# Cross attention in a decoder-like stack: normalisation, queries and attention merged into one block, with the first batch's keys and maxima among them

## The reference, cut to what matters

```
x = x + xattn_0(layernorm(x), ctx)     # Wq, bq, Wk, Wv, bv, Wo, bo
x = x + self_attention(layernorm(x))
x = x + experts(layernorm(x))
x = x + xattn_1(layernorm(x), ctx)     # no biases
x = x + mamba(layernorm(x))
x = x + expert_ffn(layernorm(x))

layernorm(x) = (x - mean) / sqrt(var + 1e-5)
xattn(q, ctx): qh = q @ Wq + bq; kh = ctx @ Wk + bk; vh = ctx @ Wv + bv
               softmax(qh kh^T / 4) vh, heads joined, @ Wo + bo
```

## Time and profile before

| | us |
|---|---|
| median of three runs (range) | 3891.38 (3885.2 to 3892.71) |
| profiled execution, its own time | 3889.54 |
| its span | 3887.8 |
| PE busy (share of the span) | 3490.9 (90%) |
| DVE busy | 2569.8 (66%) |
| ACT busy | 2155.1 (55%) |
| POOL busy | 1468.7 (38%) |
| mean granted TensorE clock | 0.940 |

### The profile page before, as it was taken

How to read it: one execution, slowest core, us unless ns; L and a number is a source line. 1 busy time by engine, 2 the same in 40 slices (tenths; PEclk the granted TensorE clock), 3 DMA queues, 4 the chain that set the end, 5 groups by cost and what they waited for, 6 DMA issues and landing times. The chain is left out here.

```text
span 3887.8 us, 136421 instructions
## 1 busy us (share of the span) xinstructions
PE 3490.9 (90%) x58106; PEld 2894.7 (74%) x58107; DVE 2569.8 (66%) x4398; ACT 2155.1 (55%) x3407; POOL 1468.7 (38%) x1389
## 2 busy tenths in 40 slices
PE   6999999999885399938999999999868899999988
PEld 4888888888674266626888888888438888888867
DVE  5777777777543122236777777777669888889864
ACT  2666666666543022204666666666447788888732
POOL 3333333333131300043333333332018888888700
PEclk8999999999996699968999999999879999999989
DMA  2001000100005201020100010000001111111100
GB/s 69 29 32 35 29 29 29 37 29 20 11 1 206 86 30 32 30 76 31 34 29 29 29 37 29 29 29 12 26 15 48 42 44 42 44 39 44 39 24 22
DMA packets 60394, 148.33 MB, mean 38 GB/s; under 512 B 8194, under 2 KB 28706, under 8 KB 59458
## 3 DMA queue, kind: packets, MB, share of 16 engines
q1 hardware_dynamic: 56770, 131.70, 10.1%
q0 software_dynamic: 3072, 8.39, 0.7%
HBM read 123.29 MB, written 16.78 MB: 36 GB/s over the span
## 5 line engine op out<-in xcount | busy, mean ns | idle before, releaser
L654 ACT ACTIVATE x_probs<-x_score_ps 128x1024 f32<-128x1024 f32 (+1 forms) x896 | 814.4, 961 | 674.5 <-PE x_score_ps L563 668.0
L714 DVE TENSOR_REDUCE x_maxes<-x_misc_ps 128x1 f32<-128x512 f32 (+1 forms) x1792 | 1022.0, 626 | 33.5 <-PE x_misc_ps L481 26.9
L678 POOL CAST x_kT_hi<-x_kT 128x512 fp32r<-128x512 f32 (+1 forms) x448 | 256.4, 572 | 1237.1 <-ACT x_kT L627 1115.3
L1965 POOL TENSOR_TENSOR b_drive<-b_b_all,b_dtx 128x1024 f32<-128x1024 f32 x256 | 602.4, 2369 | 307.2 <-DVE b_dtx L2059 183.9
L2022 DVE TENSOR_TENSOR_SCAN b_state<-b_decay_ps,b_drive 128x512 f32<-128x512 f32 x512 | 602.7, 1212 | 43.4 <-issue 18.3
L557 PE MATMUL x_score_ps<-x_qz,x_kT 32*128 32x128 f32 x13312 | 591.0, 277 | 1.8 <-issue 1.7
L557 PEld LDWEIGHTS x_score_ps<-x_qz,x_kT 32*128 32x128 f32 x13312 | 501.7, 182 | 5.0 <-issue 3.1
L531 PE MATMUL x_misc_ps<-x_probs,x_v 128*32 128x64 f32 x26624 | 464.8, 221 | 0.0
L531 PEld LDWEIGHTS x_misc_ps<-x_probs,x_v 128*32 128x32 f32 x26624 | 392.6, 110 | 65.6 <-issue 23.3
L481 PE MATMUL x_misc_ps<-x_kT_hi,x_qz_hi 32*128 32x512 f32 (+1 forms) x2048 | 423.3, 408 | 7.6 <-POOL x_kT_hi L678 3.4
L1796 PE MATMUL b_acc_ps<-ident,b_read 128*128 128x128 f32 x3072 | 414.6, 281 | 16.9 <-DVE b_xc L2045 16.9
(11 more groups left out here) (291 smaller groups left out, 5927.9 us busy)
## 6 DMA issues: line engine op xcount, KB each, us to landing
x_raw<-in_ctxT SPq DMA_DIRECT2D x64, 800.5 KB, 4.4
b_b_all<-b_b_rows SPq DMA_DIRECT2D x128, 256.0 KB, 3.3
m_w<-in_m_w SPq DMA_DIRECT2D x16, 704.0 KB, 19.4
m_w<-in_m_w SPq DMA_DIRECT2D x8, 768.0 KB, 20.2
m_slot_rows<-m_zero SPq DMA_DIRECT2D x1, 4992.0 KB, 17.1
m_block_rows<-m_slot_rows SPq DMA_DIRECT2D x39, 128.0 KB, 2.0
m_slot_out<-m_out SPq DMA_DIRECT2D x39, 128.0 KB, 1.7
x<-in_x SPq DMA_DIRECT2D x1, 2048.0 KB, 8.1
```

Of the source, the lines that this page charges most:

```text
L654: nc.scalar.activation(probs[rows, s % 2, js, 0:n], score_ps[rows, js, 0:n], ACT.Exp).then_inc(exp_done, 1)
L714: nc.vector.tensor_reduce(maxes[:, c:c + m, j, k0 // NB], bank(op)[:, 0:m * even].rearrange("p (c k) -> p c k", c=m)[:, :, 0:kn], AX.X, AL ...
L1965: nc.gpsimd.tensor_tensor(drive[:, h % 3, :, :], b_all[:, k % 2:k % 2 + 1, :].broadcast_to([P, 2, NB]), dtx[:, half * 2:half * 2 + 2, :], ...
```

## The change: what it does, and the diff

Both uses become a single block.

- SP loads x in four quarters of four tiles, each with a semaphore of its own, in the first use; the weights of keys and values, of queries, the mask, the context batches and the rest stand between and behind them.
- DVE takes statistics and normalises by quarters. ACT takes roots by quarters; it loads the table of the square root at once and that of the exponential behind the last root.
- PE transposes two tiles at a time into score_ps banks 0 and 1 (`turn_rows`), ACT copies them (`keep_rows`). Query parts go into score_ps banks 2 and 3, in order of token blocks; ACT, not DVE, scales them and adds a scaled bias (`keep_queries`). Parts 0 and 1 come first, parts 2 to 7 among the maxima.
- Four key shares are projected ahead of the first maxima; the transposes of pairs 4 to 7 stand behind the first four maxima.
- POOL splits the second context batch among the roundings, and fills only the columns of x_v that stay ones, for which only the first weighted values wait. The constants move to POOL; the memset of oT goes.
- The bias row is made in step 0, and POOL adds it to x tile by tile in steps 1 to 16 (`add_bias`).
- K, V and S operations on PE get one more wait each (w_lo_done or w_in).

```
+    AHEAD = 4
+    UT = 4; TURNS = NT // UT; PAIRS = NT // 2
+    QUERIES = [(c, blk) for blk in range(NBLK) for c in range(KD)]
+    QUERIES_AT = {0: (0, 1), 3: (2,), 4: (3,), 5: (4, 5), 6: (6, 7)}
-    PROLOGUE = (([("C",)] if bo is not None else []) + [("K", 0, 0)]
-                + [op for n in range(NG) for op in ([("K", 0, n + 1)] if n + 1 < NG else [])
-                   + [("M", 0, n, j) for j in range(QUADS)]]
+    PROLOGUE = ([("K", 0, n) for n in range(AHEAD)]
+                + [op for n in range(NG) for op in [("M", 0, n, j) for j in range(QUADS)]
+                   + ([("K", 0, n + AHEAD - 1)] if 0 < n <= NG - AHEAD else [])]
                 + [("V", 0), ("V", 1), ("K", 1, 0), ("K", 1, 1), ("T", 0)])
         def loads(sp):
+            load_x(sp, 0)
+            if source is not None:
+                sp.dma_start(ident[:, :], source[1]).then_inc(ident_in, 16)
...
+            sp.dma_start(wq_sb[:, :, :], wq).then_inc(q_in, 16)
+            sp.dma_start(bq_sb[:, :], bq).then_inc(q_in, 16)
+            sp.dma_start(mask[:, :], pair_mask).then_inc(q_in, 16)
+            load_x(sp, 1)
+            sp.dma_start(raw[:, 0, :], ctxT[0, :, :]).then_inc(ctx_in[0], 16)
+            load_x(sp, 2)
+            load_x(sp, 3)
+            sp.dma_start(raw[:, 1, :], ctxT[1, :, :]).then_inc(ctx_in[1], 16)
...
@@ tensor
+            def turn_rows(pair):
+                pe.wait_ge(xn_done, 2 * pair + 2)
+                if pair >= 2:
+                    pe.wait_ge(copied, pair - 1)
+                for j in range(2):
+                    for c in range(KD):
+                        ins = nc.tensor.transpose(score_ps[:, pair % 2, (c * 2 + j) * P:(c * 2 + j + 1) * P],
+                                                  xn[:, (2 * pair + j) % UT, c * P:(c + 1) * P], ident[:, :])
+                ins.then_inc(transposed, 1)
+            def project_queries(n):
+                c, blk = QUERIES[n]
+                pe.wait_ge(q_in, 48)
+                pe.wait_ge(copied, NB // (2 * P) * (blk + 1))
+                if n >= 2:
+                    pe.wait_ge(q_done, n - 1)
...
             def project_keys(op):
+                pe.wait_ge(w_lo_done, 1)
             def project_values(op):
+                pe.wait_ge(w_lo_done, 2)
-            pe.wait_ge(w_in, 16 * NW)
-            pe.wait_ge(const_done, 1)
-            pe.wait_ge(filled, 1)
-            if bo is not None:
-                bias_row(("C",))
+            turn_rows(0)
+            turn_rows(1)
+            for n in QUERIES_AT[0]:
+                project_queries(n)
             project_keys(("K", 0, 0))
+            project_keys(("K", 0, 1))
+            turn_rows(2)
+            turn_rows(3)
+            project_keys(("K", 0, 2))
+            project_keys(("K", 0, 3))
             for n in range(NG):
-                if n + 1 < NG:
-                    project_keys(("K", 0, n + 1))
                 for j in range(QUADS):
                     largest(("M", 0, n, j))
+                if n == 0:
+                    for pair in range(4, PAIRS):
+                        turn_rows(pair)
+                elif n <= NG - AHEAD:
+                    project_keys(("K", 0, n + AHEAD - 1))
+                if n > 0:
+                    for q in QUERIES_AT.get(n, ()):
+                        project_queries(q)
@@ scalar
+            root(0)
+            root(1)
...
+            keep_rows(0)
+            keep_rows(1)
+            root(2)
+            for n in QUERIES_AT[0]:
+                keep_queries(n)
+            keep_keys(("K", 0, 0))
+            keep_keys(("K", 0, 1))
+            root(3)
+            nc.scalar.activation(warm[:, :], std[:, 0:1], ACT.Exp, scale=-1.0)
+            keep_rows(2)
+            keep_rows(3)
+            keep_keys(("K", 0, 2))
+            keep_keys(("K", 0, 3))
...
@@ gpsimd
+            split_weights(pool)
+            for w in range(WIDE):
+                split_context(pool, 0, w)
+            pool.wait_ge(q_in, 48)
+            queries(0, qz_hi, qz_hi_done)
+            for n in range(AHEAD):
+                round_keys(0, n)
+            nc.gpsimd.memset(v_sb[:, :, :, :, DH:], 1.0).then_inc(filled, 1)
+            for n in range(AHEAD, NG):
+                split_context(pool, 1, n - AHEAD)
+                round_keys(0, n)
...
@@ vector
+            def normalise(j):
+                of = slice(j * UT, (j + 1) * UT)
+                dve.wait_ge(std_done, j + 1)
+                nc.vector.reciprocal(rstd[:, of], std[:, of]).then_inc(rstd_done, 1)
+                dve.wait_ge(rstd_done, j + 1)
+                for t in range(j * UT, (j + 1) * UT):
+                    if t >= UT:
+                        dve.wait_ge(transposed, (t - UT) // 2 + 1)
+                    nc.vector.tensor_scalar(xn[:, t % UT, :], x_sb[:, t, :], moments[:, t, 0:1], rstd[:, t:t + 1],
+                                            ALU.subtract, ALU.mult).then_inc(xn_done, 1)
+            statistics(0)
+            for j in range(1, TURNS):
+                statistics(j)
+                normalise(j - 1)
+            normalise(TURNS - 1)
             for n in range(NG):
                 for j in range(QUADS):
                     keep_max(("M", 0, n, j))
```

More of the change, by code:

```diff
@@ L215, in _, with cross_attention @@
                     ins.then_inc(transposed, 1)
[L218 to L262, removed]
+def cross_attention(nc, tag, x_sb, ident, x_sel, pair_mask, ctxT, wq, wk, wv, wo, bq, bv, bo, source=None):
     NG = (KT + 1) // 2
@@ L303, in step_ops @@
             ops.append(("V", s + 2))
+        if s == 0 and bo is not None:
+            ops.append(("C",))
         if g == NG - 1 and u + 1 < B:
@@ L356, in loads @@
                 sp.dma_start(bo_sb[:, :], bo.partition_broadcast(P)).then_inc(w_in, 16)
-            for b in range(2):
-                sp.dma_start(raw[:, b, :], ctxT[b, :, :]).then_inc(ctx_in[b], 16)
         SPLITS = [(w * NB, NB if w < WIDE - 1 else LKV - w * NB) for w in range(WIDE)]
@@ L439, in _ @@
         def _(sp):
+            loads(sp)
             for b in range(2, B):
@@ L455, in bias_row @@
                 dst = open_bank(op)
+                pe.wait_ge(w_in, 16 * NW)
                 for r in range(GROUPS):
@@ L459, in bias_row @@
                 ins.then_inc(misc_ready, 1)
+            def turn_rows(pair):
[13 more added lines that the diff above has]
+                    pe.wait_ge(q_done, n - 1)
+                for k in range(KD):
+                    ins = nc.tensor.matmul(score_ps[:, 2 + n % 2, :], wq_sb[:, k, c * P:(c + 1) * P],
+                                           xnT[:, k, blk * NB:(blk + 1) * NB], start=k == 0, stop=k == KD - 1)
+                ins.then_inc(q_made, 1)
             def project_keys(op):
@@ L606, in _ @@
                     project_values(("V", s + 2))
+                if s == 0 and bo is not None:
+                    bias_row(("C",))
                 if g == NG - 1 and u + 1 < B:
@@ L700, in _ @@
                     queries(u + 2, qz_hi, qz_hi_done)
+                if bo is not None and 0 < s <= NT:
+                    add_bias(s - 1)
                 w = g - (NG - 1 - WIDE)
@@ new lines, in statistics @@
+            def statistics(j):
+                if source is not None:
+                    dve.wait_ge(x_in[j], 16)
+                for t in range(j * UT, (j + 1) * UT):
+                    nc.vector.bn_stats(stats[:, t, :], x_sb[:, t, :]).then_inc(stats_done, 1)
+                dve.wait_ge(stats_done, (j + 1) * UT)
+                for t in range(j * UT, (j + 1) * UT):
+                    ins = nc.vector.bn_aggr(moments[:, t, :], stats[:, t, :])
+                ins.then_inc(moments_done, 1)
@@ L781, in _ @@
                     divide(("S", u - 1))
+                if s == 0 and bo is not None:
+                    keep_bias(("C",))
                 if g == NG - 1 and u + 1 < B:
```

140 lines of the change are left out of this document (98 added, 42 removed).

## The result

The kernel after takes 3866.2 us (median of four runs, 3861.34 to 3869.55), the kernel before 3890.36 beside it (four runs, 3885.2 to 3892.71): ratio 0.9939, 95% interval 0.9922 to 0.9956. That is 24.2 us less, where 44.8 were forecast, and 0.2 us outside the range. Faster was right, the size was not.

The account below looks back on a forecast made before the run. PE bounds the attention loop, so a shorter prologue moves all that follows: 25.7 us in the first use plus 19.1 in the second, 44.8 off 3889.54, gives 3844.7; with 1.8 for the median, 3847. Range 3834 to 3866.

Parts of the forecast that it names:

- Step 1, load: First-use prologue: x's quarters land at 4.5, 7.5, 11.2 and 12.7 us, the first context batch at 9.8.
- Step 2, DVE: Prologue: a quarter's statistics cost 1.62 us, normalising 0.72 + 1.45; first quarter normalised at 11.4, fourth statistics at 16.9.
- the contention: POOL's splits beside DVE's normalising: POOL held, taken as 0, upper end 3 us a use; skill's rule up to 2.9.
- Step 3, PE: Prologue: transposes end 12.8, query parts 0 and 1 at 19.0 (3.4 + 2.2), K0 to K3 with two pairs 4.0: 23.0.
- Step 4, the ring: Prologue: ACT's copies end 25.2; first four maxima products 25.5, two pairs 26.7, DVE normalises tiles 14 and 15 by 27.9.
- the forecast's last wait: Before the first maxima: only after two pairs, at 26.7, can DVE normalise tiles 14 and 15, done at 27.9.
- Steps 5 to 7: Maxima from 27.9, M0 to M3 until 38.4; query parts 2 to 7 among maxima until 54.2; V, V, K, K, T until 57.5.
- the rival of the full level: Maxima: PE rises in parts 0 and 1 and stays at full level; 55.8 us gained, 3836; chance 20%.
- the one of half level to the end: Query parts 2 to 7 among maxima never lift PE, 3.44 us each; 20 us gained, 3871; chance 17%.
- Step 8: Loop step 0, first use: the bias row's 3.75 us at half become 1.9 at full; first use 59.4 against 85.12.
- New waits in the loop: One more semaphore per K and V on PE, some 880: costs nothing; rival slower, 3935 at 100 ns each, chance 4%.
- the sum: Both prologues: 25.7 us less in the first use plus 19.1 in the second, 44.8 us; 3847.

Follow-up runs that it names:

- late fill: Kernel after, with POOL's fill of x_v moved behind the query maskings: 3862.43 us.
- splits apart: Kernel after with the late fill, and POOL's splits of the first context batch held back until the first eight tiles are normalised: 3853.8 us.
- kernel after (again): Kernel after once more, nothing edited: 3860.95 us (four runs), ratio 0.994 against the kernel before.
- query parts spread out: Kernel after, with query parts 2 to 7 one behind each maxima group from the second on, instead of from the fourth on: 3856.84 us.
- x by one DMA: Kernel after, with x loaded by one DMA of 2 MB instead of four quarters: 3870.72 us.
- late fill, spread, transposes ahead: Kernel after with late fill and query parts spread out, plus all eight pairs of transposes ahead of the first maxima products: 3849.78 us.
- the same with sixteen places: Kernel with late fill, spread, transposes ahead, plus sixteen places for normalised rows instead of four: 3851.48 us.
- the same with root and table later: Sixteen-places kernel, fourth root behind query part 0, exponential's table behind the transposes, semaphores cleared on four queues: 3832.31 us, ratio 0.9862 against kernel before.

## Why the prediction was wrong

**Step 1, load: partly.** The first quarter landed as forecast (4.79 against 4.5), the second at 9.12 instead of 7.5, the context's split began at 12.15 instead of 9.8. The sum took the middle rate of one large DMA for a queue of unlike ones. The price was small: the first quarter was normalised at 12.4 instead of 11.4. Of the 1.8 us by which K0 came late (20.8 instead of 19.0) 1.2 were there when the query parts began.

**Step 2, DVE: wrong.** A quarter of normalising was priced at 1.45 us from the earlier trace rows, where POOL was idle. Beside POOL it took 3.22, 4.05 and 4.8. The text had weighed the contention, but in one direction, and for the splits alone: it saw a POOL cast held by DVE, took 0, and set POOL's fill down nowhere. The runs with the late fill and with the splits apart show DVE held, by the fill (4.80 us instead of 2.15) and by the splits (3.22 and 4.05 instead of 1.38). Of these only the fill reached the first maximum, with 2.4 to 2.8 us in each use; what the second quarter lost beside the splits vanished in DVE's next wait, for a transpose. The Trainium skill, "GPSIMD Engine Reference", section "Key points", states that contention without a side that loses; the traces agree with it, and show both sides losing: a cast 3425 ns instead of 613, four tiles 4.80 us instead of 2.15.

**Step 3, PE: nearly right.** Query parts 0 and 1 took 6.2 us to K0 (14.64 to 20.82) instead of 5.6, within the 4.5 to 6.2 that they take in these runs; K0 to K3 with their turns took 4.2 instead of 4.0.

**Step 4, the ring: wrong by 3.7 us, the largest term.** From K0 to the first maximum the forecast was 8.9 us (19.0 to 27.9); both uses have 12.7. Within it, forecast were 2.7 us from the reading of K3's bank (25.2) to the last normalised row (27.9); it was 6.4 (27.1 to 33.5). I had two tiles left to normalise there; all four of the quarter were, since the places come free pair by pair behind the transposes of pairs 4 and 5, which ran at half level (1.91 us), and then the fill stood beside them. The experiments take this ring apart:

| from K0 to the first maximum, us | first use | second use |
|---|---|---|
| kernel after (again) | 12.68 (12.67) | 12.67 (12.66) |
| query parts spread out | 12.65 | 12.66 |
| x by one DMA | 12.66 | 12.67 |
| late fill | 9.92 | 10.24 |
| late fill, splits apart | 9.91 | 9.97 |
| late fill, spread, transposes ahead | 8.51 | 8.52 |
| the same with sixteen places | 8.44 | 8.45 |
| the same with root and table later | 7.12 | 7.07 |

The fill is 2.4 to 2.8 us of the miss and the place of the transposes in the order 1.4 to 1.7; together they are more than all of it. The four places for normalised rows, which the forecast's last wait was built on, cost nothing once the transposes stand ahead. The first maximum came at 33.5 (32.2 again) against 27.9, and 26.6 us after the second statistics against 21.8; 1.8 and 1.0 of these misses lie ahead of K0, in the load and in parts 0 and 1.

**Steps 5 to 7: right.** From the first maximum to step 0's maxima were forecast 29.6 us. The profile has 29.3 in the first use (33.50 to 62.84) and 29.3 in the second, with the level falling and rising where it was put: part 2 at 3.76 us, part 3 at 1.98. So the rival of the full level fell: the level went down at 27.7 although the longest idle piece of PE between the query parts and this moment is 1.15 us; the one of half level to the end fell too, although its time, 3871, was nearer than mine: by luck, since no query part behind part 2 ran at half level.

**Step 8: right.** The bias row took 1.89 us in step 0. The forecast priced the new order as a whole, and not what falls away: taken out of the kernel before one at a time, the bias gave 4.5 us and the fill 7.5 and 8.8. No run has both; if they add up, quarters and merged order are the first use's remaining 10 us.

**New waits in the loop: right.** The steps have a median of 4.18 or 4.19 us in before and after; nothing was lost to 880 waits.

**What the sum left out.** It ended at the two prologues, and called the boundaries part of what falls away. What was lost outside it: the longer clearing, 2.1 us; the issue of the expert weights, 2.1, through the place that three DMAs more, 1200 us earlier, give its long ones; 4.6 in the self attention and 2.4 in the first loop. One stop of PE in step 91, 3.4 us (last section), covers the loop's share. The self attention's I can't lay on the change: its middle part took 137.7 to 146.7 us in four executions without the change and 140.9 to 149.4 in nine with it.

So of the 19.9 us missing in the profiled execution 5.4 lie in the first prologue, 4.8 in the second, 2.1 in the clearing, 2.1 in the issues of the expert weights, and 5.5 in PE's stop and in stretches that vary.

## What to carry to other kernels

When an operation is moved beside another engine's, price both at their held times, look in both directions, and then ask whether the held operation is what the path waits for; a fill that nobody waits for is still not free if it lies beside DVE's reads. A merged block has more semaphores, and its end grows with them: clear them on several queues. To compare prologues, measure between two events inside them: from K0 to the first maximum four executions agree to 0.03 us, while first maxima differ by over 1 us through the load and the level. And before a large reordering, try the one wait that a trace shows: the fill alone gave 16.3 of the 36.5 us of the two prologues.

## What the runs showed that was not expected

PE stopped for 1.4 to 1.6 us in the middle of a loop in several executions, waiting for nothing that the profile shows, and mostly the level fell behind it. Timeline, then window, of the kernel after in step 91, which took 7.40 us instead of 4.0:

```profile
455.98 0.50 PE L592 MATMUL x_score_ps<-x_shift,x_ones 1*128 1x512 f32 x2 [1.63 <-issue]
```

```profile
458.00:460.00 2.00, 2.00 (x48) 1.66 (x49) 0.42 (x1) 0.65 (x2) 0.62 (x1) 0.50 0.00 0
```

In that step the same stop stands in six of the nine executions with the change: where the level fell behind it the step took 7.11 to 7.40 us, and 5.63 in the two (late fill, one load) where it held. Without it the step takes 4.00. It is not in the kernel after's second execution, and in none of the four without the change, but these have such stops elsewhere: step 35 of the kernel before's second execution (7.36), step 175 of the second use in its first (7.16). So single executions of one kernel differ by some 3 us for each.

The traces hold a lead. In all nine stops of over 1.3 us in the loops of the thirteen executions a transfer of 16 KB on the queue called "q8 instruction" had begun 2.2 to 2.5 us before PE went on, and it came 7.4 to 8.2 us after the one before it, where the median is 4.8. That queue makes 454 such transfers in the kernel after, one for 256 of PE's 116213 matmuls and weight loads, so it seems to bring PE its instructions. But there are late ones without a stop (7.38 us at 453.92 in the kernel after's second execution), so that PE ran out of instructions is an argument, not shown.
